# A gated RWKV and MLP block: the recurrence without its running maximum and in PSUM, the program unrolled in slots of 16 matmuls

## What is computed

```python
k = layernorm(x);  v = ctx                      # over the channels
# WKV: a recurrence over t for each channel, with decay w and bonus u
p, q, o = 0, 0, -1e38
for t in range(1024):
    no = max(o, u + k[t]); A = exp(o - no); E = exp(u + k[t] - no)
    y[t] = (A * p + E * v[t]) / (A * q + E)
    no2 = max(w + o, k[t]); A2 = exp(w + o - no2); E2 = exp(k[t] - no2)
    p, q, o = A2 * p + E2 * v[t], A2 * q + E2, no2
x2 = x + tanh(g_xattn) * y
d = gelu(f16(layernorm(x2)) @ W0.T + bias0)     # W0: 4096 x 1024, kept as float32
out = x2 + tanh(g_ffn) * f16(f16(d) @ W1.T + bias1)
```

## Time and profile before

| | |
|---|---|
| three runs | 2144.49, 2145.67, 2146.55 us, median 2145.67 |
| the profiled execution, first to last instruction (the page gives no other time of it) | 2146.2 us |
| PE busy, DVE busy | 88%, 51% of the span |
| ACT busy, POOL busy | 27%, 28% |
| mean granted PE clock | 0.939 |
| chain that ended last | PE 68%, DVE 17%, issue 8%, POOL 3%, DMA 2%, ACT 1% |
| DMA | 286.56 MB, 134 GB/s on average |

### The profile page before, as it was taken

One profiled execution on the slowest core, in us unless ns is written; L12 is line 12 of the kernel. 1 busy time (PEld: TensorE's weight loads), 2 busy tenths in 40 slices (PEclk: granted clock), 3 DMA queues, 4 the chain that ended last, 5 costly groups with the idle time before them and its releaser, 6 DMA issues.

```text
span 2146.2 us, 23175 instructions
## 1 busy us (share of the span) xinstructions
PE 1888.6 (88%) x8960; PEld 892.4 (42%) x8960; DVE 1103.5 (51%) x1250; ACT 586.7 (27%) x759; POOL 592.7 (28%) x394
## 2 busy tenths in 40 slices
PE   1046778978889997999999997999999999999999
PEld 1023334434434443444444443444444444444444
DVE  8979975998971148899311158899211000000000
ACT  3326553343433232443000133443000121110000
POOL 4636750455653122444000022444000000000000
PEclk6558889989989998999999998999999999999999
DMA  5424574535466434333333333333233322223331
GB/s 176 142 103 156 168 254 169 212 119 205 164 229 197 156 117 139 108 126 126 122 118 118 138 128 118 127 127 140 90 115 118 108 79 79 79 88 112 108 110 53
DMA packets 72285, 286.56 MB, mean 134 GB/s; under 512 B 7680, under 2 KB 7680, under 8 KB 65024
## 3 DMA queue, kind: packets, MB, share of 16 engines
q1 hardware_dynamic: 72192, 285.28, 37.8%
HBM read 218.14 MB, written 67.11 MB: 133 GB/s over the span
## 4 chain that ended last, share of the span: by engine, by line
PE 68%; DVE 17%; issue 8%; POOL 3%; DMA 2%; ACT 1%; SPq 0%; DVEq 0%; POOLq 0%; ACTq 0%
PE acc L921 36%; PE acc L893 29%; DVE uOE L734 3%; DVE uOE L731 2%; DVE uOE L703 2%; DVE uA L712 1%; PE trA L856 1%; PE trA L872 1%; DVE uR L717 1%; DVE uOE L727 1%; DVE uR L722 1%; DVE K L745 1%; DVE uOE L709 1%; DVE uR L741 1%; DMA xin<-x_in 1%
## 5 line engine op out<-in xcount | busy, mean ns | idle before, releaser
L893 PE MATMUL acc<-XT,W 128*128 128x512 f16 x4096 | 911.7, 385 | 60.4 <-ACT DT L533 52.5
L921 PE MATMUL acc<-DT,W 128*128 128x512 f16 x4096 | 900.1, 381 | 12.1 <-POOL W L411 12.1
L893 PEld LDWEIGHTS acc<-XT,W 128*128 128x128 f16 x4096 | 405.8, 99 | 554.5 <-issue 66.7
L921 PEld LDWEIGHTS acc<-DT,W 128*128 128x128 f16 x4096 | 401.5, 98 | 491.1 <-issue 23.4
L757 DVE SCALAR_TENSOR_TENSOR xo<-e,tg,xo 128x512 f32<-128x512 f16 x64 | 52.1, 814 | 626.8 <-ACT e L542 626.6
L533 ACT ACTIVATE DT<-acc,b 128x512 f16<-128x512 f32 (+1 forms) x256 | 173.1, 686 | 511.2 <-PE acc L893 510.9
L542 ACT ACTIVATE e<-acc,b 128x512 f16<-128x512 f32 x64 | 43.8, 684 | 676.8 <-PE acc L921 676.8
L378 POOL TENSOR_TENSOR rstd<-rstd,power 128x1 f32<-128x1 f32 x64 | 47.5, 742 | 611.8 <-DVE rstd L646 611.8
L741 DVE RECIPROCAL uR<-uR 128x512 f32<-128x512 f32 x64 | 209.6, 3314 | 0.0
L391 POOL TENSOR_TENSOR uOE<-uOE,uV 128x512 f32<-128x512 f32 x64 | 81.0, 1275 | 380.4 <-ACT uOE L502 233.7
L640 DVE BATCH_NORM_STATS2 stats<-trA 128x6 f32<-128x512 f32 x60 | 38.8, 689 | 218.8 <-PE trA L872 218.8
(11 more groups left out here) (54 smaller groups left out, 1000.2 us busy)
## 6 DMA issues: line engine op xcount, KB each, us to landing
W<-parts_dram SPq DMA_DIRECT2D x56, 2048.0 KB, 8.1
parts_dram<-W SPq DMA_DIRECT2D x64, 512.0 KB, 6.7
stage<-w_in SPq DMA_DIRECT2D x52, 512.0 KB, 6.0
uV<-vT_in SPq DMA_DIRECT2D x64, 256.0 KB, 2.7
xT<-xT_in SPq DMA_DIRECT2D x32, 512.0 KB, 5.2
x_dram<-K SPq DMA_DIRECT2D x32, 512.0 KB, 3.7
xo<-x_dram SPq DMA_DIRECT2D x32, 512.0 KB, 9.6
out<-xo SPq DMA_DIRECT2D x32, 512.0 KB, 7.9
```

The lines of the kernel that those rows point to most:

```text
L893: mm = nc.tensor.matmul(acc[bank][:, :], W[:, slot, part, q, P * c:P * (c + 1)], XT[:, c, HALF * half:HALF * (half + 1)], start=(c == 0 an ...
L921: mm = nc.tensor.matmul(acc[bank][:, :], W[:, slot, part, q, P * c:P * (c + 1)], DT[:, nb, HALF * half:HALF * (half + 1)], start=(nb == 0 ...
```

## The change

**Recurrence.** The running maximum goes. With wp = max(w, 0), the layernormed tile gets -t * wp added (`norm_x`, a second pass over the tile on DVE), so that exp gives terms that only need the decay exp(min(w, 0)), a constant of the channel. A unit is now (`unit` on DVE, seven instructions of 512 elements and up to three tiny ones): PE transposes four 128x128 blocks of `xin` into a PSUM bank; ACT replaces them by their exponential E in place; DVE writes E * V into the second bank of the pair, runs two scans whose one input is the constant decay, forms denominator and numerator in PSUM (E * bonus + q, EV * bonus + p), the reciprocal, and the gated quotient; POOL adds x (`residual`). K, its copies by ACT and three of POOL's four operations are gone. Units no longer go in pairs.

**PSUM.** 3 banks for the products instead of 4, two pairs of banks (`front`) for units and for the transposes of x2, one bank for the f16 transposes. In the first 8 units a third pair is made of two product banks.

**Order.** No loops: each engine walks over 4 x 128 slots, each of 16 matmuls (a quarter of a group in the second product). Tables say before which slot a unit or a step of a layernorm stands. SP loads the next x of a unit (`load_xT(n + 4)`) at the slot of unit n and waits there for the residual of unit n. Constants are loaded from ACT's queue, with a 512 KB row of w, and DVE prepares them before its first layernorm. Four tiles of x are loaded at once.

```diff
-BANKS = 4
+BANKS = 3
...
+    for i, k in enumerate((5, 6, 9, 12, 14, 17, 20, 22)):
+        UNIT_SLOT[CB + i] = k
+    for i, k in enumerate((37, 38, 41, 44, 46, 49, 52, 54, 64, 65, 68, 71, 73, 76, 79, 81)):
+        UNIT_SLOT[UNITS + i] = k
+    for i in range(HT):
+        LN1_SLOT[HT + i] = 1 + i
+        LN1_SLOT[2 * HT + i] = 33 + i
+        LN1_SLOT[3 * HT + i] = 60 + i
+        LN2_SLOT[HT + i] = (27 + i, 29 + i)
+    for i in range(TILES):
+        LN2_SLOT[TILES + i] = (88 + 2 * i, 90 + 2 * i)
...
+        for i, k in enumerate((1, 4, 8, 12, 16, 20, 24, 28, 37, 40, 44, 48, 52, 56, 60, 64)):
...
+        for i in range(TILES):
+            LN2_SLOT[T + i] = (at + 72 + 6 * i, at + 75 + 6 * i)
...
+            def load_xT(n):
+                b, i = divmod(n, UNITS)
+                if n >= 4:
+                    sp.wait_ge(x2_done, n - 3)
...
+                        if NB <= k < 2 * NB - Q and k % Q == 0:
+                            load_parts((k - NB) // Q + 1, k)
...
+                    for n in UNITS_AT.get(K, ()):
+                        if n + 2 < UNITS * B:
+                            load_v(n + 2)
+                        if n % UNITS < UNITS - 4:
+                            load_xT(n + 4)
...
+                nc.scalar.activation(bank, bank, ACT.Exp, bias=shift[:, n % CB:n % CB + 1]).then_inc(e_ready, 1)
...
+                    if b == 0 and k < NB - 2 * Q:
+                        hi_piece(k + 2 * Q)
...
+            def norm_x(T):
...
+                nc.vector.scalar_tensor_tensor(row, grow[:, :], negt[:, T % TILES:T % TILES + 1], row,
+                                               ALU.mult, ALU.add).then_inc(xn_ready, 1)
...
+            def unit(n):
...
+                if i < CB:
+                    nc.vector.tensor_scalar(state[:, i, 0:1], V[:, j, 0:1], SEED, None, ALU.mult)\
+                        .then_inc(begun, 1)
+                nc.vector.tensor_copy(S[:, j, :, 0], state[:, i, :]).then_inc(seeded, 1)
+                nc.vector.tensor_tensor(EV, E, V[:, j, :], ALU.mult).then_inc(ev_done, 1)
+                nc.vector.tensor_tensor_scan(S_q[:, 1:], decay[:, c:c + 1].to_broadcast([P, HALF]), E,
+                                             S_q[:, 0:1], ALU.mult, ALU.add).then_inc(q_done, 1)
+                nc.vector.tensor_tensor_scan(S_p[:, 1:], decay[:, c:c + 1].to_broadcast([P, HALF]), EV,
+                                             S_p[:, 0:1], ALU.mult, ALU.add).then_inc(p_done, 1)
+                nc.vector.scalar_tensor_tensor(E, E, bonus[:, c:c + 1], S_q[:, 0:HALF], ALU.mult, ALU.add)\
+                    .then_inc(den_done, 1)
+                nc.vector.scalar_tensor_tensor(EV, EV, bonus[:, c:c + 1], S_p[:, 0:HALF], ALU.mult, ALU.add)\
+                    .then_inc(num_done, 1)
+                if i < CB:
+                    nc.vector.tensor_copy(state[:, i + CB, :], S[:, j, :, HALF]).then_inc(saved, 1)
+                nc.vector.reciprocal(S_q[:, 0:HALF], E).then_inc(rec_done, 1)
+                nc.vector.scalar_tensor_tensor(S_q[:, 0:HALF], EV, tg[:, 0:1], S_q[:, 0:HALF],
+                                               ALU.mult, ALU.mult).then_inc(y_done, 1)
...
+            def residual(n):
...
+                nc.gpsimd.tensor_tensor(slot, slot, S[:, n % 2, 1, 0:HALF], ALU.add).then_inc(x2_done, 1)
...
+            def unit(n):
...
+                pe.wait_ge(y_done, n - 1 if n >= CB else n - 2)
+                for j in range(HT):
+                    mm = transpose_piece(n, j)
+                mm.then_inc(kt_done, 1)
```

More of the change, by code:

```diff
@@ L45 @@
 STEPS = NB // Q
-assert STEPS == CB == 8 and TILES == 8
 GROUPS1 = 2 * NB
 GROUPS = GROUPS1 + 2 * CB
-BANKS = 4
+SLOTS = 4 * NB
+BANKS = 3
+RING1, RING2 = 5, 3
 EPS = 1e-5
-NEG_INF = -1e38
-R_CAP = 60.0
 W_SCALE = 1024.0
[L56 to L67, removed]
@@ new lines, with group_of, ring_slot @@
+place_front()
+UNITS_AT = {k: [n for n in UNIT_SLOT if UNIT_SLOT[n] == k] for k in set(UNIT_SLOT.values())}
+LN1_AT = {k: T for T, k in LN1_SLOT.items()}
+X2T_AT = {k[0]: T for T, k in LN2_SLOT.items()}
+X2_AT = {k[1]: T for T, k in LN2_SLOT.items()}
+def group_of(b, k):
+    if k < GROUPS1:
+        return GROUPS * b + k
+    return GROUPS * b + GROUPS1 + (k - GROUPS1) // Q if k % Q == Q - 1 else None
+def ring_slot(g):
+    if g < NB:
+        return g % RING1, g // RING1
+    slot = (g - NB) % RING2
+    return slot, (g - NB) // RING2 + len(range(slot, NB, RING1))
@@ L119, in build @@
         xo = sb("xo", [P, 2, L])
[L122 to L135, removed]
@@ L203, in store_x2, with load_x @@
[L203 to L212 removed]
+            def load_x(T):
+                half, slot = T // HT, T % HT
+                if half:
+                    sp.wait_ge(kt_done, CB * half)
+                sp.dma_start(xin[:, slot, :], x[T]).then_inc(x_landed[slot], 16)
@@ L603, in _ @@
-            second_product(0, FRONT_M0, split=True)
-            def first_product(b, front=True):
-                def step(s, tiles, pair):
-                    for q in range(Q):
-                        for half in range(2):
-                            i = 2 * q + half
-                            gelu(GROUPS * b + 2 * Q * s + i, Q * s + q, half, i % BANKS)
-                            if i in (1, 2) and tiles is not None:
-                                copy_k(b + 1, tiles + i - 1)
-                            if i == 3 and pair is not None:
-                                exps(b + 1, pair)
-                for s in range(HT):
-                    step(s, 2 * s if front else None, s - 1 if front and s else None)
-                with act.Fori(HT, STEPS) as s:
-                    step(s, None, s - 1 if front else None)
@@ new lines, in _ @@
+            pe.wait_ge(s_pool0, 6)
+            for j in range(HT):
+                pe.wait_ge(xn_ready, j + 1)
+                for n in range(3):
+                    mm = transpose_piece(n, j)
+                    if j == HT - 1:
+                        mm.then_inc(kt_done, 1)
+            for n in range(3, CB):
+                unit(n)
+            for T in range(HT):
+                tokens_x2(T)
+                if T:
+                    channels_x2(T - 1)
+            channels_x2(HT - 1)
```

1054 lines of the change are left out of this document (392 added, 662 removed).

## The result

| | before | after |
|---|---|---|
| median of 4 runs | 2145.08 us (2144.11 to 2146.55) | 1994.29 us (1993.89 to 1995.2) |
| ratio, 95% interval | | 0.9296 (0.9282 to 0.931) |
| span of the profiled execution | 2146.2 us | 1992.6 us |
| mean granted PE clock | 0.939 | 0.993 |
| PE, DVE busy | 88%, 51% | 93%, 43% |

The account below looks back on a forecast made before the run. DVE's recurrence bounds the kernel before 151 us, PE held up through ACT until about 740, then PE. Head 123, rest of batch 0 489.5, batches 1 and 2 921.4, batch 3 446.7 sum to 1980.6; forecast 1980, range 1960 to 2030.

Parts of the forecast that it names:

- What bounds it: Kernel before: DVE's recurrence before 151 us, PE held up by it through ACT until about 740, PE from there on.
- batches 1 and 2: Middle batches: 460.7 us each, 459.7 of work plus one for the start, together 36 us less than before.
- Scans at 1.18, reciprocal 3.25, PSUM operands at no price: DVE's unit: these times per instruction, with terms in PSUM not slowing it, sum to 8.9 us a unit.
- The fourth rival: DVE units: PSUM operands slow every instruction, 14.9 us a unit beside POOL, 2175 us in all; chance 0.02.
- A unit of 9.1 us in the head: Before the products: DVE takes 9.1 us a unit with POOL light, 73 us for eight units.
- 27 to 28 us ahead of the units: Start of the head: loads, constants and their preparation, layernorm and its second pass take 27 to 28 us.
- Slots 5 to 27, 8 us of stall: Batch 0, units of the second half: ACT paces; 6 us for late x2 and 2 for pieces SP issues late.
- `load_parts` of slot 40 ... 4: Batch 0, slots 37 to 54: this load stands behind unit 17's residual; 4 us of wait and 1.8 of clock.
- Slots 60 to 81: Batch 0: layernorm behind `lo_piece` at slot 64, 2 us; units beside POOL and `add_out`, 2 us.
- The third rival: Batch 0, slots 1 to 24: SP and DMA pace, 22 us more, some weight loads late, 2006 us; chance 0.12.
- The second rival: DVE paces: POOL contention or PSUM operands make a unit 11 us, 2034 in all; 2000 at 10 us; chance 0.17.
- The signs: Trace if right: products at 118 to 128, scans near 1.25, small PE gaps, 460 us middle batches, no gap from 1534.

Follow-up runs that it names:

- e8: Kernel before the change with its reciprocal left out and the quotient replaced by min(uA, den): 2092.73 us, ratio 0.9752.
- e2: Changed kernel with the 128x2 copy that seeds a unit's scans split into two copies of 128x1: 1988.98 us.
- e11: Changed kernel with both 128x2 copies of a unit, seed and saved state, split into two copies of 128x1: 1987.27 us.
- e1: Changed kernel with load_xT(n + 4) and store_x2(n - 1) issued on SP five slots after unit n: 1977.07 us.
- e6: Changed kernel with each unit's reciprocal issued twice, with the same result: 2093.77 us, ratio 0.9759.
- e7: Changed kernel with the reciprocal left out, so the quotient uses the denominator itself: 1948.61 us.
- e12: Changed kernel with late SP loads and stores, both copies narrowed, SP loads held until constants land, two tiles' statistics before the wait for constants: 1960.17 us.
- e3: Changed kernel with the seed of unit n + 1 copied before the reciprocal of unit n: 1995.77 us.
- e10: Changed kernel with late SP loads and stores, seed before reciprocal, SP loads held until constants land, two tiles' statistics before the wait for constants: 1965.44 us.
- e4: Changed kernel with SP issuing units' x and weight pieces only after the constants have landed: 1992.65 us.

## Why the prediction was right, and where it was off

- **What bounds it.** Right: DVE's recurrence ahead of the products, PE held through ACT and SP until about 390, PE alone from there. The last batch, batches 1 and 2 (461.61 and 460.71 against 460.7) and the PE work in batch 0 came as worked out.
- **Scans at 1.18, reciprocal 3.25, PSUM operands at no price.** Right: a unit from 161.37 to 169.82, whose copies meet no operation of POOL, takes 8.45 us against 8.9. The fourth rival, PSUM operands that slow DVE, is excluded by 1254 to 1270 ns a scan and 727 to 751 a `scalar_tensor_tensor`. The Trainium skill ("SBUF — State Buffer", who interferes with whom) held for scans with the constant decay in SBUF and their terms in PSUM. It is PSUM that frees them, not the constant: L703 of the kernel before reads a constant too, but K in SBUF, and beside POOL's pieces two of it took 4.19 us instead of 2.45 (e8, at 71.34).
- **A unit of 9.1 us in the head.** Off: 9.7, and 8 x 0.6 = 5 us. The step was "9.1 a unit with POOL light": the seed copy stands exactly where the residual of the unit before runs on POOL and waits it out each time, in the units beside `lo_piece` and in those without it. The 9.7 that the prediction kept for units beside `lo_piece` is the same number for another reason. e2 and e11 take 4.6 and 6.2 us from the head.
- **27 to 28 us ahead of the units.** Off by 2 (29.98): constants at 13.91. The tiles of x2 took 18.9 us instead of 21, which gives these 2 back.
- **Slots 5 to 27, 8 us of stall.** The mechanism was right: ACT paces, and slot 27 begins 104.6 us after the first matmul (232.74) where the prediction had 104. PE is idle there for 4.1 us, not 8: part of what was put down as a stall is the first 80 matmuls at the lower clock, 20.12 us instead of 17.44, costed at 1.8, and the 2 us for late pieces did not come.
- **"`load_parts` of slot 40 ... 4".** The step that was most off. The mechanism, SP in order behind a residual, was right for slot 40 (4.54), but the prediction followed it for one load only. The two after it stand behind later units in the same way: 1.47 and 5.95, so 12.0 instead of 4. Each of the longer two is followed by matmuls at the lower clock, 1.5 and 2.5 us, where 1.8 was set for one. Slots 60 to 81, costed at 4, gave some back: from 387.61 PE is idle for 1.15 of 236 us. Batch 0 is 6 us over in all, and that it is no more is partly luck: 8 us more of waits for weights, 3 more of clock and 2 more of PE's own work (470.4, estimated as its 477.0 busy less 6.6 of lower clock, against 468.5) stand against 4 and 3 us of stalls that did not come.
- **The sum.** Head +5, batch 0 +6, batches 1 and 2 +1 make the span 1992.6 instead of 1980.6. The other 2 of the 14 are between span and time: the profiled execution took 1994.41, where the prediction set the time 0.5 under the span, as of before.
- **The third rival** (SP and DMA pace, 2006) was partly right. The sign that the prediction set for it, PE waiting for DMA of weights more than 10 us in sum, came: 12.0; and "two or three loads of weights come late like that of slot 40" is what happened. Its main cost was wrong: in the first half of batch 0, where it put 22 us, 251 GB/s were moved, ACT waited once for a piece, 1.4 us, and PE never did. The waits came in the second half, at 209 GB/s, and e1 removes two of the three without moving a byte less.
- **The second rival** (11 us a unit) did not come, but e6 shows its price: 3.35 us a unit cost 99.5, so the 1.9 it supposed would have cost some 56 (an estimate, scaled), near the 54 that the prediction set; e7, where 3.34 us less gave only 45.7, shows that such scaling is rough. Its 2000 for units of 10 us is 2003 by its own terms (8 x 0.9 in the head and three phases of 7.2 - 2).
- **The signs.** First matmul at 118 to 128 (128.10, at the edge), scans near 1.25, 460 us per middle batch and no gap from about 1534 on all came; of the gaps of 1 to 5 us the largest was 5.95, and three loads of parts released PE, not one.

What stays open: e1, the narrow copies and the start of the head are told apart; of the last 20 us that e12 gains behind slot 32 not each was taken apart, and the loss of e3 in the first half was seen, not undone by itself. The 53 us that the new order gives at the old length of a unit (e6) are one sum, not taken apart. e1 alone keeps a wait of 4.17 us for weights that e10 and e12 do not have; which of their other edits removes it is not known.

## What to carry to other kernels

Once PE paces, what is left lies in the order of an in-order queue: look at each load that is needed soon and ask which wait stands ahead of it, for all of its repeats and not only the first. A stage that alternates between engines in pairs hides two bounds; shortening one (e8) shows the other, and a reordering that removes both at once gains more than the work that it saves. An operation of nearly no work can still wait for a whole operation of another engine; narrowing it can cost less than finding a free place for it.

## What was not expected of the hardware

- An fp32 copy of 128x2 on DVE waits until a POOL operation that is running has ended (1.10 and 1.28 us beside an addition, 2.11 beside a weight piece), while 128 copies of 128x1 never took over 0.155 us.
- The same is seen in wide operations of the kernel after: the first pass of `norm_x` (L472), of 804 ns in the median of 32, takes 2612 at 144.35, and the second (L478), with two SBUF inputs, 3142 instead of 1284 at 140.76, both beside POOL's weight piece.
- DVE in PSUM: reciprocal out of PSUM 3347 ns against 3314 from SBUF before; statistics out of PSUM 688 ns for 512 elements against 682 from SBUF. Neither is dearer by more than 1%. A normalisation out of PSUM, 1344 ns (L489) against 804 from SBUF (L472), is.
- Constants issued on ACT's queue landed at 13.91 us while SP's queue issued several MB of other loads, and at 11.72 when SP waited for them (e4).
